# Two layer-norm scalings move from VectorE to ScalarE, and GpSimd makes their negated means

## The reference

```python
h = tok(x, ...)                                        # gather, add, layer norm
h = h + attention_1(_layernorm(h), ...)                # feature-map attention
h = h + prototypes(_layernorm(h), ...)                 # 2 of 32 low-rank experts by distance
h = h + attention_2(_layernorm(h), ...)                # causal attention with rotary positions
h = h + feed_forward(_layernorm(h), ...)               # ternary weights, relu
```

## Time and profile before

| | |
|---|---|
| median of three runs | 471.68 us (469.02 to 472.74) |
| the profiled execution's own time | 469.25 us |
| its span, first to last instruction | 467.4 us |
| mean granted TensorE clock | 0.96 of 2.4 GHz |
| HBM read, written | 11.80 MB, 2.36 MB |

### The profile page before, as it was taken

One profiled execution on the slowest core, in us unless ns is written; L12 is line 12 of the kernel. 1 busy time (PEld: TensorE's weight loads), 2 busy tenths in 40 slices (PEclk: granted clock), 3 DMA queues, 4 the chain that ended last, 5 costly groups with the idle time before them and its releaser, 6 DMA issues.

```text
span 467.4 us, 13967 instructions
## 1 busy us (share of the span) xinstructions
PE 398.8 (85%) x5026; PEld 272.7 (58%) x5026; DVE 356.4 (76%) x892; ACT 257.3 (55%) x573; POOL 285.4 (61%) x399
## 2 busy tenths in 40 slices
...
GB/s 137 187 280 184 159 92 16 88 104 75 123 117 82 117 114 106 95 123 94 136 117 116 107 84 123 82 130 109 117 97 128 112 108 79 97 36 24 13 13 35
DMA packets 145843, 48.55 MB, mean 104 GB/s; under 512 B 137264, under 2 KB 143216, under 8 KB 145776
## 3 DMA queue, kind: packets, MB, share of 16 engines
...
HBM read 11.80 MB, written 2.36 MB: 30 GB/s over the span
## 4 chain that ended last, share of the span: by engine, by line
PE 34%; POOL 20%; issue 16%; DVE 12%; DMA 10%; ACT 4%; SPq 2%; another core or an unknown queue 1%; POOLq 0%; DVEq 0%; ACTq 0%
PE PS L1416 12%; PE PS L2005 4%; DMA rTm<-split 4%; DMA qkT<-qs 3%; PE PS L1926 3%; PE PS L2023 3%; DVE split L1074 2%; POOL wneg L617 2%; POOL hgs L682 2%; POOL qe L667 1%; POOL split L696 1%; PE PS L1627 1%; POOL emb L597 1%; PE PS L1911 1%
## 5 line engine op out<-in xcount | busy, mean ns | idle before, releaser
L1074 DVE TENSOR_REDUCE split<-PS 128x16 f16<-128x2048 f32 x16 | 36.7, 2297 | 10.6 <-PE PS L1495 8.0
L693 POOL TENSOR_TENSOR stage_f<-stage_f 128x512 f32<-128x512 f32 x16 | 21.0, 1311 | 26.7 <-DVE stage_f L1062 10.6
L1156 ACT ACTIVATE xTR<-PS 128x256 f16<-128x256 f32 x16 | 6.1, 384 | 48.9 <-PE PS L1806 48.8
L2005 PE MATMUL PS<-xTM,w1q 128*128 128x128 f16 x512 | 31.4, 219 | 0.0
L2005 PEld LDWEIGHTS PS<-xTM,w1q 128*128 128x128 f16 x512 | 28.6, 98 | 3.6 <-issue 3.6
L667 POOL TENSOR_TENSOR qe<-qef,qe 128x704 f16<-128x704 f32 x16 | 24.9, 1554 | 6.9 <-ACT qe L1265 2.4
L1768 PE MATMUL PS<-faT_hi,hgT 128*128 128x256 f16 x128 | 25.4, 286 | 3.0 <-DMA hgT<-hgs 2.8
L686 POOL TENSOR_TENSOR rstdR<-mvR,consts 128x1 f32<-128x1 f32 x16 | 8.9, 555 | 29.9 <-DVE mvR L1034 29.8
L1416 PE MATMUL PS<-rwqk_hi,xTR 128*128 128x512 f16 x64 | 25.9, 449 | 0.3
L1416 PE MATMUL PS<-wqkT_hi,xTP 128*128 128x512 f16 x64 | 24.3, 422 | 1.4 <-DVE xTP L897 1.4
L1439 PE MATMUL PS<-warm 128*128 128x512 f16 x98 | 23.1, 401 | 1.4 <-DVE warm L1123 1.4
...
## 6 DMA issues: line engine op xcount, KB each, us to landing
...
rT<-split SPq DMA_TRANSPOSE x26, 3.6
```

The costliest lines, as they stand in the source:

```text
L693: g.tensor_tensor(rot[:, :, :].rearrange("p h d -> p (h d)"), rc[:, :], rs[:, :], ALU.add).then_inc(rot_ok, 1)
L1074: v.tensor_reduce(slots(SLOT - DH)[:, 0:H, DH - 1].rearrange("p (c j) -> p j c", j=4), PS[:, BANK["s1"]:BANK["s1"] + 4, :].rearrange("p j ...
L1156: return a.activation(dst, src, ACT.Copy)
L2005: last = pe.matmul(PS[:, BANK["m1"] + f // 4, f % 4 * P:(f % 4 + 1) * P], w1q[:, n % KC, f * P:(f + 1) * P], xT["M"][:, n, :], start=False ...
```

## The change

The DVE list loses all 16 `Fxn` and all 16 `Rxn`; what remains keeps its order. The ACT list gains them; what was there keeps its order. Lists of POOL, PE and SP are the same. On POOL the steps `Frs` and `Rrs` have one instruction more each. The new `Fxn` of ACT stands directly behind these operations:

| tile | 0 | 1 | 2 | 3 | 4 | 5 | 6 | 7 | 8 | 9 | 10 | 11 | 12 | 13 | 14 | 15 |
|---|---|---|---|---|---|---|---|---|---|---|---|---|---|---|---|---|
| `Fxn` behind | ym1 | Rhi | ke | ex2 | ex2 | ex1 | ex1 | Exn | ex2 | Rhi | ex1 | ke | ex2 | oh | ex2 | Rhi |
| `Rxn` behind | ym3 | qe2 | qe2 | Mxn | vr | qe2 | qe1 | Exn | Pxn | qe1 | vr | qe2 | qe1 | qe1 | vr | hgTa |

In tiles 5 and 6 ACT has `ex2` ahead of `ex1`, so `Fxn` stands behind both halves there too; in tile 10 it stands between them. `Rxn` is always directly ahead of `Rhi`. `Fxn` is always directly ahead of `Fhi` or of `xsq`.

```diff
     "DVE": """
...
-        zr3 Est ctl qmx Pst qb Eag od on qd oV kmx hP Fst Fag Pag kmr zr1 kb Fxn kd zm zf3 FT nd2 top zt Est tix Eag qlo gap Pst gt hg ctl zth od Pag
+        zr3 Est ctl qmx Pst qb Eag od on qd oV kmx hP Fst Fag Pag kmr zr1 kb kd zm zf3 FT nd2 top zt Est tix Eag qlo gap Pst gt hg ctl zth od Pag
...
@@ POOL, step Frs; Rrs likewise
                     g.tensor_tensor(rstd["F"][:, :], mv["F"][:, 1:2], consts[:, :], ALU.pow).then_inc(rs_ok["F"], 1)
+                    g.wait_ge(rs_ok["F"], t + 1)
+                    g.tensor_scalar(nmean["F"][:, :], mv["F"][:, 0:1], rstd["F"][:, 0:1], -1.0, ALU.mult, ALU.mult)\
+                        .then_inc(nm_ok["F"], 1)
@@ DVE
                 elif op == "Fag":
                     wait(v, ag_ok["F"], 2 * t + 1)
-                    wait(v, xn_ok["F"], t)
+                    wait(v, nm_ok["F"], t)
                     v.bn_aggr(mv["F"][:, :], stats["F"]).then_inc(ag_ok["F"], 1)
-                elif op == "Fxn":
-                    wait(v, rs_ok["F"], t + 1)
-                    wait(v, tr_ok["F"], t)
-                    wait(v, xsq_ok, t)
-                    v.tensor_scalar(xn["F"][:, :], h_of(t), mv["F"][:, 0:1], rstd["F"][:, 0:1], ALU.subtract, ALU.mult).then_inc(xn_ok["F"], 1)
...
-                    wait(v, xn_ok["R"], t)
+                    wait(v, nm_ok["R"], t)
...
-                elif op == "Rxn":
-                    wait(v, rs_ok["R"], t + 1)
-                    wait(v, tr_ok["R"], t)
-                    v.tensor_scalar(xn["R"][:, :], h_of(t), mv["R"][:, 0:1], rstd["R"][:, 0:1], ALU.subtract, ALU.mult).then_inc(xn_ok["R"], 1)
@@ ACT
+                elif op == "Fxn":
+                    wait(a, nm_ok["F"], t + 1)
+                    wait(a, tr_ok["F"], t)
+                    wait(a, xsq_ok, t)
+                    normalise(xn["F"][:, :], h_of(t), "F")
...
+                elif op == "Rxn":
+                    wait(a, nm_ok["R"], t + 1)
+                    wait(a, tr_ok["R"], t)
+                    normalise(xn["R"][:, :], h_of(t), "R")
```

More of the change, by code:

```diff
@@ L81 @@
[L81 to L92, removed]
@@ new lines @@
+        on ws hgTb diag oV qmx qb qd hF hP Rst Fst Rag kmx Fag zr2 kmr zq1 kb RT kd FT qlo rs1 nd2 rs2 top rc tix zq2 gap ctl gt ws hg od on
+        zq3 rT2b rT1b diag qmx oV qb ngm qd hF Rst Rag hP Est Fst kmx Fag kmr RT kb kd Pst Eag rc rs2 FT rs1 Pag nd2 top qlo zq4 gap tix ctl
+        gt hg od ws on diag rd qmx qb ro qd ngm Est rV hF Rst Rag hP kmx hR Fst Fag kmr RT Eag kb Pst kd rs1 rc FT rs2 Mst nd2 top qlo tix Pag
+        gap Mag gt ctl hg rd ws diag od ro on qmx qb Est qd ngm Eag rV hF Rst hP Rag kmx hR Fst Fag kmr RT kb Mst kd rc rs2 FT rs1 Est nd2 top
@@ new lines @@
+        qb Eag qd ob ngm hF Rst Rag Pst hP hR kmx RT Fst Pag Fag kmr Mst Mag kb rs2 rs1 rc kd FT Est nd2 top qlo tix rd ro Eag gap Pst gt diag
+        hg ml1 ws ml2 qmx ctl qb qd ob od on ngm hF Rst hR Rag kmx Est hP Pag Fst kmr Eag Fag kb kd RT FT Pst rs1 nd2 top rs2 rc Mst gap tix
+        qlo Pag Mag gt rd hg ws ctl ro diag ml1 od ml2 on qmx qb qd ob ngm hF Rst Rag kmx hP hR Fst Fag kmr RT kb kd FT rs1 Mst nd2 top Mag
+        tix rs2 rc gap qlo rd ctl gt hg diag Est Eag od ws ro on qmx ml1 qb ml2 qd ob ngm hF Rst Rag hP Fst hR kmx Fag RT kmr Pst kb kd rc Mst
```

35 lines of the change are left out of this document (13 added, 22 removed).

## The result

The changed kernel took 476.97 us, the median of four runs (473.39 to 478.76), and the kernel before 470.93 us beside it (469.02 to 472.74). The ratio is **1.0212, with an interval of 1.016 to 1.0264**: slower by some 2%. The time forecast was 479.0 us, in a range of 471 to 487. A second comparison of the same two kernels, run later as an experiment, gave 1.0254 (1.0172 to 1.0337). The ratios leave out executions taken for disturbed, in e7 for instance four of six, so the experiments' table has the ratio of the medians of all executions beside them.

What follows compares the result with a forecast made beforehand. No engine was full: DVE and POOL set the pace in the first 100 us, then PE. The terms for R, F, first tiles, POOL, givebacks and clock summed to +9.8 us on 469.25, giving 479.0 us, range 471 to 487.

Steps and rivals of the forecast that it cites:

- F: Prototype rows: `Fxn` queued on ACT makes `Ftr` late; +3.7 us at five tiles, +3.9 at tiles 11, 13, 7, 2.
- The scaling itself: ACT takes 594 ns per scaling, 1.0 us from `rstd` to `xn`; DVE loses 23.0 us of busy time.
- R: Second attention's rows: -2.1 us at five tiles, +0.7 at four, +2.4 at tile 8, +1.0 around tile 14.
- What is given back: PE's lateness eats waits of the scores `s1` for DMA and DVE: between 0 and 6.1 us, taken as -3.0.
- the ramp's 0.8: POOL's four added negated means in tiles 0 and 1: between 0 and 1.5 us, taken as +0.8.
- The first tiles: Tile 0: `Ftr` behind `ym1` starts 2.4 us late, 1.7 absorbed before `prt`, +0.7 stays; POOL's means add +0.8.
- The negated means on POOL: Added POOL instructions: +0.8 us in tiles 0 and 1; the remaining 28 hidden in POOL's idle time, 0.
- The clock: New PE stalls bring none to four more slow-clock stretches, 0 to 6.8 us; one taken, +1.7.
- The relief of DVE: DVE's freed time gives nothing beyond the gains at `Rxn`, since PE sets the pace: 0.
- Absorbed: Rival: DMA waits eat PE's lateness and DVE's later operations come early; +3.5 us, about 473 us; chance 0.19.
- Cascade: Rival: three or four slow-clock stretches, late `qk` or `hg` return as DMA waits; +18, 487 us; chance 0.12.
- Faster: Rival: DVE is the hidden pacemaker, its scalings slowed by overlapping POOL work; 457 us at the utmost, some 464; chance 0.07.

Runs made afterwards that it cites:

- e7: Changed kernel with 13 of the 32 scalings further forward in ACT's order; ratio to the kernel before 0.9849, median 465.46 us.
- e5: The changed kernel measured once more, against the kernel before: ratio 1.0254, median 476.54 us.
- e1: Kernel before with only `Fxn` and its negated mean moved, `Rxn` left on DVE: ratio to the kernel before 1.0229, median 479.25 us.
- e2: Kernel before with only `Rxn` and its negated mean moved, `Fxn` left on DVE: ratio to the kernel before 1.0031, median 470.64 us.
- e6: Changed kernel with products on a zero tile filling PE's waits ahead of `Ftr` at nine more tiles: ratio to the kernel before 1.0172, median 474.23 us.
- e4: Changed kernel, with DVE also making both scalings into a tile nobody reads: ratio to the kernel before 1.0306, median 481.82 us.
- e9: `Fxn` on ACT at e7's early places, `Rxn` on DVE, both negated means on POOL: ratio to the kernel before 1.0071, median 470.08 us.
- e11: The kernel of e7 measured again, against the kernel before: ratio 0.9882, median 465.14 us.

## Why the prediction was right, step by step

**The number.** The forecast was +9.8 us on a base of 469.25. Measured were +6.0 by the medians beside each other (470.93 and 476.97), and +8.3 by the means of all executions. Beside the medians the change was forecast 3.8 us too large and the base lay 1.7 us too low, and the two errors partly cancel in 479.0 against 476.97.

**The mechanism** was right. `Fxn` queues behind the exponentials, PE stands ahead of line 1696 (now 1686) for ACT at eleven tiles and 11.6 us; at least ten and 8 were forecast (8.4 at ten tiles in e5). e1 and e2 put the loss on F, and e7 on the place in the queue.

**The scaling itself.** 594 ns forecast, 596 and 598 in the mean; 1.0 us from `rstd` to `xn`, 1.00 in tile 11. The relief of DVE was 19.4 us of busy time, not 23.0.

**F.** The five common tiles (3, 4, 5, 12 and 14) were forecast at 0.6, 0.5, 0.8, 0.9 and 0.9. PE stood 0.40, 0.40, 0.90, 0.90 and 0.90: 3.5 against 3.7. At tiles 7 and 13 it stood 0.74 and 1.28, against 0.85 and 1.4. Tile 2 stood 1.08 and not 0.1. At tile 1 a wait of 1.18 us for DVE's scaling went away, which had no part in the sum. Tile 11, forecast at 1.6, shows no wait in this trace, and 1.20 in e5 and e1. Here `Ftr` started 2.1 us later than before (323.07 against 320.96), when `Rtr` ahead of it was 0.2 behind (317.62 against 317.40), and the clock did it: behind the wait of 1.05 us at that `Rtr` and two shorter ones the granted clock is 0.61 from 320 to 324 us (it was full before). The same product before and after:

```profile
319.89 0.38 PE L1416 MATMUL PS<-rwqk_lo,xTR 128*128 128x512 f16 x1
```

```profile
320.80 0.63 PE L1406 MATMUL PS<-rwqk_lo,xTR 128*128 128x512 f16 x1
```

The products from `rqk` to `Ftr` took 2.67 us instead of 1.30.

**R.** The gains came where they were named, and in size: PE's wait fell by 0.65, 0.63 and 0.63 us at tiles 1, 11 and 13, and rose by 0.14 or 0.15 at tiles 5, 7, 9 and 15. Tile 8 lost 2.36, tile 14 1.05. But four tiles were mis-sized: tile 0, set at nothing because POOL's chain was to set the pace, stood 2.22 us; tile 10, a gain of 0.2, lost 0.85; tiles 12 and 3, with PE busy anyway, lost 1.02 and 0.36. Tile 10 differs between executions (0.19 in e5), the others don't by much, except tile 3, which shows no wait in e5. By the prediction's own test (more than 8.7 us without tile 8), the sum for R was too good: it was 14.4 - 2.9 = 11.5 us. I took PE's arrival from the old trace at each tile; once PE's order around a tile has moved, an operation that was never waited for can be late.

**What is given back.** This is the term that was most wrong. I took 3.0 us, at `s1`. `s1` gave 0.4 (DMA 4.3 to 3.9; 4.3 again in e5). `s2`, just ahead of `Rtr` or just behind it, gave 4.0 (2.0 in e5), and its row had no part in the sum. Counted alike, the forecast had 12.0 us of new waits (10.3, and the 1.7 that it took off at `prt`) and 4.7 given back (3.0 and the same 1.7); the trace has 13.9 and 6.7, that of e5 9.6 and 6.6. The forecast's net was 8.1 with the ramp's 0.8, the traces have 7.2 and 3.0. That the sum fits is partly luck: the given-back term was too small in both traces, and only in one did larger new waits make up for it.

**The first tiles.** `Ftr` of tile 0 started at 60.78, 60.96 was forecast. Of the 2.26 us, 1.8 and not 0.7 was left at `prt` (63.97 against 62.17). Here too it was the clock: after PE had stood 3.41 us ahead of that `Ftr`, it was 0.57 from 60.7 to 64.2, where the kernel before had 1.00.

```profile
60.78 0.69 PE L1686 MATMUL PS<-ident,xnF 128*128 128x128 f32 x2 [3.41 <-ACT xnF L1140]
...
61.69 0.63 PE L1406 MATMUL PS<-wqkT_lo,xTP 128*128 128x512 f16 x1
```

The products from `qk` to `prt` took 2.70 us instead of 1.68, and that is nearly all of the 1.1 us by which the term was too small. By `Rtr` of tile 2 the changed kernel was level with the kernel before (124.64 against 125.04). The clock is in this as well: from 100 to 108 us it was 0.57 in the kernel before and 1.00 in the changed one.

**The negated means on POOL**, set at +0.8 in the first tiles: the means alone cost nothing (0.989 and 0.998), and where DVE keeps the scaling they help it. The term was set too high for a reason that the durations in the earlier trace rows already hinted at.

**The clock.** +1.7 forecast. The test that I had set (a mean clock that stays at 0.96) would call the term wrong in the profiled execution, which had 0.967. Over ten executions it was 0.955, over 69 of the kernel before 0.962, which goes with some 2.7 us. The size fits, and what a fallen clock costs is shown at tiles 0 and 11: 1.0 and 1.4 us, each behind a new stall. But low stretches also went away elsewhere (100 to 108 and 294 to 300 us), so one pair of traces can't show that the change lowers the clock in the mean, and e6 supports it in direction only. Read in steps of 2 us, the stretches after 100 us in which it fell were six in the kernel before, not the five that I counted, and five in the changed one.

**The relief of DVE**, set at nothing: e4 lies 3.6 us above the changed kernel at an equal clock, with a standard error of 1.2, but the two profiled executions take the same time. It may have been worth something.

**The rivals.** *Absorbed* was half right: about half of the new waits were taken up (6.7 of 13.9, 6.6 of 9.6 in e5), but PE's idle time still grew. *Cascade* was right about one sign and wrong about the size. It had `hg` return as a DMA wait, and the product with `hgT` waited 2.8 us for its DMA before and 5.3 after; e5 has 3.3, though, so this is not shown to be the change's doing. *Faster* named the right mechanism for DVE's slow scalings and the half (R) that lost nothing, and failed on F. A time below the kernel before came once the scalings stood early on ACT; that it came by less lock between DVE and GpSimd was not tested.

**Open:** why e9 is slower than e7 and e11; why `s2` waits between 3.9 and 10.2 us for its DMA in these kernels; how much of the clock's change the stalls cause; whether DVE's load reaches the end at all.
